# Head of a fused layer kernel: projection weights loaded in halves by two queues, other loads behind them, and the later tiles' normalisation moved

## The chip, the cores and the metric

One core of one Trainium2 chip. The metric is the device time of one launch in microseconds; everything, weights included, starts in HBM. The kernel before takes 723.18 us (median of 3 runs, 723.03 to 726.49).

## The reference, cut to what matters

An attention layer with fast weights, followed by a mixture-of-experts layer; x has 2048 rows of 256, all is fp32.

```
xn  = layernorm(x)                        # per row, 16 tiles of 128 rows
qkv = xn @ Wqkv ; small = xn @ [Wlr|Wm|Ws]  # one weight tile "wall", 820 columns with the gate's
for each of 16 chunks (128 rows), one after the other, carrying W0,W1,W2 and momenta:
    out   = W1 . (silu(W0 q) * (W2 q))          # with the weights as they stand
    dW0, dW1, dW2 from k, v and learning rates  # "key side", gradients
    M = dW + M * mean(momentum)
    W = renorm(W + newtonschulz5(M))            # 5 iterations of X X', A A, B X
windowed attention (128 back) beside it; sum of both @ Wo
feed-forward on xn: gate logits, top groups and experts, 8 of 32 experts per row,
    one shared expert (up, relu^2, down), sorted rows per expert group, fc2
output = x + attention part + feed-forward part
```

## The kernel before, in words

Five engines run five instruction streams written out by hand; they meet at semaphores, each engine in strict order. SP and ACT issue the DMAs, each on a queue of its own.

`body(i)` is the step of chunk i (0 to 15), and exists in every engine's stream. It has the key side (`k_side`), the query side (`q_side`, `q_gate`), gradients (`grads`, `grad`), the norm of the momentum (`sums`, `sum_copy`, `ss_pow`, `x_first`), and then 20 steps "st": four for each of 5 Newton-Schulz iterations. In st 0, 4, 8, 12, 16 something is turned or nothing is done, in st 1, 5, ... TensorE makes the Gram products and VectorE `Am` (`ns_a`), in st 2, 6, ... TensorE squares and VectorE makes `Mp` (`ns_m`), in st 3, 7, ... TensorE applies and ACT copies the new `XX` (`ns_x`). A dictionary `fill` says which other work an engine does after its part of a step: in st 4 the output norm (`q_norm`), in st 5 to 12 the projections and norms of chunk i+1 (`prep_...`), in st 11 to 17 attention. The last instructions renormalise the fast weights and turn them (`turn_w`, `w_T`), and the next chunk's key side waits for that.

Layer norm goes by groups n = 0 to 8: tile 0 alone, then tiles 2n-1 and 2n, last tile 15. For a group VectorE takes statistics (`ln_stats`, L1314 ff.), GpSimd raises variance+eps to the power -0.5 (`prep_rstd`, L431), VectorE makes the shift (`ln_shift`, L1337), ACT applies (`ln_apply`, L587), TensorE turns the result (`ln_turned`, L873), ACT copies it to `xnT_all` (`ln_xnT`, L595). `ln_turn(i, k, half)` places the turning in one of the slots of body 0: k counts 8 pairs of slots (`y_slot`, half 0; `h_slot`, half 1) among the steps. After each turning ACT applies the next group at once. `gate_pair(i, k, half)` places the router's eight groups of matmuls (`gate_rows`, TensorE; `gate_out`, ACT) in the same slots; the router's sort starts in body 1. Expert work fills the slots of later bodies.

Before body 0 stands the head, the same preparations for chunk 0: `ln_stats(0)`, `ln_first`, `ln_turned(0)`, `turn_w(0, g)`, then the projection (`prep_qk`, `prep_v`), silu, the norms of q and k by `prep_n8` (GpSimd) and `prep_qkn`, learning rates (`lr_a`, `lr_b`, `lr_c` around ACT's exp and ln, which lie in another table than sigmoid), the window copies and `prep_kl` (GpSimd). VectorE starts with 13 memsets, and the statistics of groups 1 to 4 are taken in the head, those of 5 to 8 in body 0. TensorE waits for `wall` and `rows` (bias rows) before the projection, and for all of the feed-forward weights before body 0.

Of the kernel before, what the change touches and what calls it, by code (L numbers as in the profile page):

```python
# [27 lines left out]
ALU = mybir.AluOpType  # L28
# [58 lines left out]
def build(nc, x, wall_d, rows_d, wo, fast_d, affine_d, fc1T, fc2T, e1T, e2T, upT, downT, ident_d, fixed_d, out):  # L87
# [10 lines left out]
    with ExitStack() as ctx:  # L98
# [170 lines left out]
        def per_group(name):  # L269
# [4 lines left out]
        e_const, e_later, e_ffn_w, e_ttw, e_init = (sem(n) for n in (  # L274
            "first_const_in", "later_const_in", "ffn_weights_in", "fast_weights_in", "init"))
# [33 lines left out]
        NCONST, NLATER, NFFN = 2, 3, 5  # L309
# [37 lines left out]
        def gate_pair(i, k, half):  # L347

            order = {(0, 1, 0): 0, (0, 2, 0): 1, (0, 3, 0): 2, (0, 4, 0): 3, (0, 5, 0): 4, (0, 6, 0): 5, (0, 7, 0): 6, (1, 0, 0): 7}
            return order.get((i, k, half))  # L350
# [5 lines left out]
        def _(sp):  # L356
            xv = x.rearrange("(t p) d -> p t d", p=P)
            sp.dma_start(x_all[:, 0, :], x[0:P, :]).then_inc(e_x0, 16)
            sp.dma_start(ident[:, :], ident_d[:, :]).then_inc(e_ident, 16)
            for dst, src in ((wall[:, :, :], wall_d[:, :, :]),  # L360
                             (rows[:, :], rows_d.partition_broadcast(P))):
                sp.dma_start(dst, src).then_inc(e_const, 16)
            sp.dma_start(x_all[:, 1:5, :], xv[:, 1:5, :]).then_inc(e_x1, 16)
            for dst, src in ((fixed[:, :, :], fixed_d[:, :, :]), (affine[:, :, :], affine_d[:, :, :]),
                             (wo_s[:, :, :], wo.rearrange("(k p) n -> p k n", p=P))):
                sp.dma_start(dst, src).then_inc(e_later, 16)
            sp.dma_start(x_all[:, 5:NT, :], xv[:, 5:NT, :]).then_inc(e_x2, 16)
            sp.wait_ge(e_init, 2)
# [54 lines left out]
        def _(pool):  # L423
# [94 lines left out]
            def body(i, last):  # L518
# [6 lines left out]
                k_u(i, 1)  # L525
                move(i, "key side", 4)
# [8 lines left out]
                if first:  # L535
                    fill[13] = [restore_mask]
                    for n, st in ((5, 1), (6, 4), (7, 6), (8, 8)):
# [19 lines left out]
            for g in range(G):  # L557
                row_pow(0, g)
            prep_n8(0)
            for n in range(1, 5):  # L560
                prep_rstd(n)
            window(0)
# [9 lines left out]
        def _(act):  # L572
            for g in range(G):
                act.dma_start(Wn[g][:, :, :], fast_d[g]).then_inc(e_ttw, 16)
            for dst, src in ((gf_s[:, :, 0:P], fc1T.rearrange("(k p) n -> p k n", p=P)),
                             (gf_s[:, :, P:P + E], wall_d[:, :, 3 * D + GATE:3 * D + SMALL]),
# [1383 lines left out]
```

## Time and profile before

| | |
|---|---|
| median of 3 runs | 723.18 us (723.03 to 726.49) |
| profiled execution | 722.96 us, its span 721.2 us |
| busy: TensorE / its weight load | 637.7 us (88%) / 527.1 us (73%) |
| busy: VectorE, ScalarE, GpSimd | 551.8 (77%), 386.8 (54%), 232.1 us (32%) |
| chain that ended last, by engine | PE 40%, DVE 36%, ACT 10%, POOL 6%, issue 5%, DMA 1% |
| DMA over the span | 75.52 MB, mean 105 GB/s |

PE is TensorE, PEld its weight load, DVE VectorE, ACT ScalarE, POOL GpSimd, SP the engine that only issues DMAs. Times in rows are microseconds from the start of the span; the 1.8 us between the span and the execution's own time lie around it. A row of a timeline can merge instructions that follow each other; what stands in brackets is how long the engine was idle just before and what ended that. No single engine is full and the chain runs over all of them, so what counts is which one ends last at each place.

### The profile page before, as it was taken

How to read it: one execution, taken by the hardware profiler on the slowest of the kernel's cores; microseconds unless marked ns; L12 is line 12 of the kernel's file. 1: busy time of each engine (PE TensorE's matmuls, PEld its weight loads, DVE VectorE, ACT ScalarE, POOL GpSimd, SP SyncE). 2: the span in 40 equal slices, each digit the busy share in tenths (PEclk: the TensorE clock that was granted, in tenths of full speed). 3: DMA queues.
4: the chain of work that ended last, by engine and by line, in shares of the span. 5: the costliest groups of instructions: out<-in, count | busy, mean ns of one | idle time of the engine just before them, and what ended most of it. 6: DMA issues, size and time to landing. Idle time of an engine off the chain costs nothing.

```text
span 721.2 us, 24642 instructions
## 1 busy us (share of the span) xinstructions
PE 637.7 (88%) x10081; PEld 527.1 (73%) x10081; DVE 551.8 (77%) x1878; ACT 386.8 (54%) x938; POOL 232.1 (32%) x296
## 2 busy tenths in 40 slices
PE   4688789878998899999999999999999999998865
PEld 2566577766776678878787887888878888786654
DVE  5876877798576687978879787897888878768554
ACT  2576353543553546656475665747647566452533
POOL 1522113117773221313113222131312213158730
PEclk9799979999999999999999999999999999998988
DMA  8300000220111125354454444454454553011211
GB/s 271 150 3 2 2 2 3 78 101 32 46 37 55 65 79 182 127 163 142 153 187 155 159 166 145 153 185 145 148 172 139 170 193 113 23 28 38 73 48 59
DMA packets 40160, 75.52 MB, mean 105 GB/s; under 512 B 9712, under 2 KB 24432, under 8 KB 40048
## 3 DMA queue, kind: packets, MB, share of 16 engines
q1 hardware_dynamic: 36224, 68.08, 29.0%
q0 software_dynamic: 2048, 4.33, 2.0%
q8 instruction: 80, 1.31, 0.7%
q10 hardware_dynamic: 1776, 1.54, 0.7%
q14 instruction: 32, 0.26, 0.1%
HBM read 64.73 MB, written 9.20 MB: 103 GB/s over the span
## 4 chain that ended last, share of the span: by engine, by line
PE 40%; DVE 36%; ACT 10%; POOL 6%; issue 5%; DMA 1%; SPq 0%; DVEq 0%; POOLq 0%
PE CC L860 13%; PE HB L860 9%; PE YB L860 8%; DVE hb L1782 6%; PE M L860 6%; ACT hb L583 3%; POOL r L429 3%; POOL xsrc L454 3%; ACT XX L583 3%; DVE Am L1485 2%; DVE sq L1497 2%; DVE Mp L1491 2%; DVE Wn L1503 1%; PE CC L1011 1%; DVE comb L1601 1%
## 5 line engine op out<-in xcount | busy, mean ns | idle before, releaser
L429 POOL TENSOR_TENSOR r<-r,half 128x3 f32<-128x3 f32 (+1 forms) x78 | 81.5, 1050 | 181.7 <-DVE r L1361 96.7
L583 ACT ACTIVATE hb<-HB 128x512 f32<-128x512 f32 x86 | 51.3, 597 | 67.4 <-PE HB L860 66.2
L583 ACT ACTIVATE XX<-CC 128x384 f32<-128x384 f32 (+1 forms) x150 | 63.1, 459 | 34.8 <-PE CC L860 33.9
L1782 DVE TENSOR_TENSOR hb<-hb,cwb 128x512 f32<-128x512 f32 x70 | 76.5, 1093 | 6.8 <-ACT hb L583 5.8
L860 PE MATMUL HB<-xsT,e_s 128*128 128x128 f32 x560 | 78.3, 283 | 1.7 <-issue 1.7
L860 PE MATMUL YB<-e_s,hb 128*128 128x128 f32 x560 | 77.4, 281 | 0.0
L860 PEld LDWEIGHTS YB<-e_s,hb 128*128 128x128 f32 x560 | 69.3, 191 | 7.1 <-issue 4.3
L860 PEld LDWEIGHTS HB<-xsT,e_s 128*128 128x128 f32 x560 | 67.9, 191 | 4.6 <-issue 1.8
L860 PE MATMUL CC<-XX,Mp 64*64 64x64 f32 x1800 | 63.2, 229 | 8.0 <-DVE Mp L1491 8.0
L860 PE MATMUL CC<-Am 64*64 64x64 f32 x1800 | 53.6, 236 | 18.1 <-DVE Am L1485 17.3
L860 PEld LDWEIGHTS CC<-Am 64*64 64x64 f32 x1800 | 41.4, 138 | 35.0 <-DVE Am L1485 29.9
L1491 DVE SCALAR_TENSOR_TENSOR Mp<-CC,rests 128x192 f32<-128x192 f32 x150 | 47.7, 353 | 25.0 <-PE CC L860 24.0
L860 PEld LDWEIGHTS CC<-XX,Mp 64*64 64x64 f32 x1800 | 50.7, 137 | 18.4 <-DVE Mp L1491 11.3
L1485 DVE TENSOR_TENSOR Am<-CC,shifts 128x192 f32<-128x192 f32 x150 | 47.5, 351 | 16.5 <-PE CC L860 14.8
L860 PE MATMUL M<-wall,xnT_all 128*128 128x512 f32 (+1 forms) x128 | 55.7, 541 | 2.2 <-DMA rows<-in_rows 1.4
L583 ACT ACTIVATE hb<-hb 128x512 f32<-128x512 f32 x86 | 54.0, 628 | 1.4
L860 PE MATMUL CC<-Mp,XX 64*64 64x64 f32 x1440 | 47.0, 223 | 0.3 <-issue 0.3
L478 POOL COPY akT<-akT 128x256 f32<-128x256 f32 x15 | 7.6, 505 | 122.9 <-issue 122.9
L429 POOL TENSOR_TENSOR r<-r,neghalf 128x4 f32<-128x4 f32 x16 | 16.2, 1011 | 88.9 <-DVE r L1545 88.9
L583 ACT ACTIVATE XT<-CC 128x256 f32<-128x256 f32 x30 | 11.3, 385 | 60.1 <-PE CC L958 60.1
L860 PEld LDWEIGHTS CC<-Mp,XX 64*64 64x64 f32 x1440 | 39.7, 139 | 0.4 <-issue 0.4
L860 PE MATMUL CC<-XX 64*64 64x64 f32 x1440 | 38.0, 231 | 2.0 <-ACT XX L583 2.0
(249 smaller groups left out, 1504.1 us busy)
## 6 DMA issues: line engine op xcount, KB each, us to landing
e_s<-in_e1T SPq DMA_DIRECT2D x35, 512.0 KB, 4.7
e_s<-in_e2T SPq DMA_DIRECT2D x35, 512.0 KB, 5.8
cwb<-tile_weights SPq DMA_DIRECT2D x35, 512.0 KB, 3.7
sorted_rows<-e_s SPq DMA_DIRECT2D x5, 476.0 KB, 9.8
xs<-sorted_rows SPq DMA_DIRECT2D x35, 68.0 KB, 5.5
sorted_out<-yo SPq DMA_DIRECT2D x35, 64.0 KB, 3.0
out<-xnT_all SPq DMA_DIRECT2D x8, 256.0 KB, 2.2
x_all<-in_x SPq DMA_DIRECT2D x1, 1408.0 KB, 14.7
```

Source lines behind the costliest of these rows:

```text
L429: return pool.tensor_tensor(dst, src, expo[:, 0:n], ALU.pow)
L454: pool.indirect_dma_start(xsrc[:, t, j, 0:P], None, y_d[:, :], bass.IndirectOffsetOnAxis(ap=dest_i[:, t, j:j + 1], axis=0)).then_inc(e_gat ...
L478: pool.tensor_copy(akT[:, :, 0, :], akT[:, :, 1, :])
L583: return nc.scalar.activation(out_, in_, func, **kw)
L860: return pe.matmul(out_, lhsT, rhs, start=start, stop=stop)
L1011: ins = pe.transpose(CA[g][0:HD, w * P:(w + 1) * P], Wn[g][:, w, :], ident[:, :])
L1485: nc.vector.tensor_tensor(Am[g][:, :, :], SQUARED[g] if it and g else PROD[g], shifts[:, it, :].unsqueeze(1).to_broadcast([P, 3, HD]), ALU ...
L1491: nc.vector.scalar_tensor_tensor(Mp[g][:, :, :], SQUARED[g] if it and not g else PROD[g], NS[it][2], rests[:, it, :].unsqueeze(1).to_broad ...
L1497: nc.vector.tensor_tensor(sq3[g][:, :, :], Wn[g][:, :, :], Wn[g][:, :, :], ALU.mult).then_inc(e_up[g], 1)
L1503: nc.vector.tensor_tensor(Wn[g][:, :, :], Wn[g][:, :, :], X[g][:, :, :], ALU.add).then_inc(e_up[g], 1)
L1601: nc.vector.tensor_tensor(comb[:, :], att[:, :], ttt[:, :], ALU.add).then_inc(e_comb, 1)
L1782: nc.vector.tensor_tensor(hb[u % RING][:, :, :], hb[u % RING][:, :, :], gate, ALU.mult).then_inc(e_hw, 1)
```

## The change

- **Loads.** `wall` is loaded in two halves (by its k index, 410 KB each), one on SP's queue behind tile 0 of x, one on ACT's queue ahead of the fast weights. The identity and `rows` stand behind SP's half. SP then waits until both halves have landed and issues everything else, the feed-forward weights too, which ACT issued before. TensorE waits for the halves only; `rows` is waited for by VectorE.
- **VectorE's start.** Four memsets (`akT`, `vw`, `beat`, `zero`) go behind the first normalisation and the Newton-Schulz constants; no engine waits for them until GpSimd's first window copy and SP's blank writes. The first statistics no longer wait for the memsets.
- **Head.** ACT loads the sigmoid table right after its three DMA issues. GpSimd does the window copies before the norms' power. The statistics of group 2 stand at the end of the head, those of 3 and 4 in body 0. VectorE copies the turned q and k (`first_qkT`) in place of ACT, and ACT applies group 1 behind its key side and gate sigmoid. Constants of the sort go to body 0, st 10.
- **Body 0.** Groups 1 to 8 are turned in the second halves of slots 0 to 7 (before: both halves of slot 0, then slots 1 to 6). ACT's `ln_apply` of groups 3 to 8 stands at fixed steps and no longer follows each turning; statistics and shifts are spread over st 0 to 17. TensorE does the first projection matmul of chunk 1 behind the momentum's sums. The router's eight groups go one slot later, (0,2) to (1,1).

```diff
 def ln_turn(i, k, half):
-    order = {(0, 0): 1, (0, 1): 2, (1, 1): 3, (2, 1): 4, (3, 1): 5, (4, 1): 6, (5, 1): 7, (6, 1): 8}
+    order = {(k, 1): k + 1 for k in range(PER)}
 def gate_pair(i, k, half):
-    order = {(0, 1, 0): 0, (0, 2, 0): 1, ..., (0, 7, 0): 6, (1, 0, 0): 7}
+    order = {((n + 2) // PER, (n + 2) % PER, 0): n for n in range(NT // 2)}
 # SP
 sp.dma_start(x_all[:, 0, :], x[0:P, :]).then_inc(e_x0, 16)
+sp.dma_start(wall[:, 0, :], wall_d[:, 0, :]).then_inc(e_wall, 16)
 sp.dma_start(ident[:, :], ident_d[:, :]).then_inc(e_ident, 16)
-wall, rows -> e_const ; x tiles 1-4 ; fixed, affine, wo ; x tiles 5-15
-sp.wait_ge(e_init, 2)
+rows -> e_const
+sp.wait_ge(e_wall, 32)
+x tiles 1-4 ; affine, fixed, wo ; gf_s (2) ; x tiles 5-15 ; up_s, down_s, fc2_s
+sp.wait_ge(e_init, 3)
 # GpSimd
 body(i): k_u(i, 0); k_u(i, 1)
+    if first: prep_rstd(2)
-    for n, st in ((5, 1), (6, 4), (7, 6), (8, 8)):   prep_rstd(n)
+    for n, st in ((3, 1), (4, 4), (5, 7), (6, 10), (7, 13), (8, 15)):   prep_rstd(n)
 head: prep_rstd(0); row_pow(0, g)
-    prep_n8(0); prep_rstd(1..4); window(0); prep_kl(0)
+    pool.wait_ge(e_init, 3); window(0); prep_n8(0); prep_rstd(1); prep_kl(0)
 # ACT
+act.dma_start(wall[:, 1, :], wall_d[:, 1, :]).then_inc(e_wall, 16)
 fast weights
-gf_s (2), up_s, down_s, fc2_s
+act.preload_act_table_set("sigmoid_and_others")
 extra(i, k, half):  ln_xnT(n)
-    if n < NL - 1: ln_apply(n + 1)
+    if n == 1: ln_apply(2)
 body(i): k_side(i, 0); k_side(i, 1); gate_sig(i)
+    if i == 0: ln_apply(1)
+    if i == 0:
+        fill[7], fill[8] = [prep_small(m), prep_sq8(m), y_slot(i, 3)], []
+        ln_apply(n) for n, st in ((3, 2), (4, 5), (5, 9), (6, 12), (7, 16), (8, 18))   # 9, 12: first in the step
 head:
-    w_T(0, g); prep_vT(0); table exp/ln; lr_exp(0); prep_qkT(0); lr_ln(0); table sigmoid; ln_apply(1)
+    w_T(0, g); prep_vT(0); table exp/ln; lr_exp(0); lr_ln(0); table sigmoid
 # TensorE
-body: prep_qk(m); sums(i, 0); sums(i, 1)
+body 0: sums(0, 0); sums(0, 1); prep_qk(m)
 head:
-pe.wait_ge(e_const, 16 * NCONST)
+pe.wait_ge(e_wall, 32)
 # VectorE
-beat, zero, akT, vw memset at the start; dve.wait_ge(e_init, 2)
+def blanks():   akT, vw, beat, zero memset, then e_init
+def first_qkT():
+    dve.wait_ge(e_pnqk, 1)
+    nc.vector.tensor_copy(qkT, M1).then_inc(e_qkT, 1)
 body 0:
+    ln_shift(2) ahead of x_first
-    ln_stats (5, 0), (6, 2), (7, 4), (8, 6);  ln_shift (5, 2), (6, 4), (7, 6), (8, 8)    # (group, st)
+    ln_stats (3, 0), (4, 2), (5, 6), (6, 8), (7, 12), (8, 14)
+    ln_shift (3, 2), (4, 5), (5, 9), (6, 12), (7, 14), (8, 17)    # shifts first in the fill
+    fill[10] += sort_consts
 head:
+    blanks() behind ns_consts()
-    ln_stats(1); ln_stats(2); prep_qkn; lr_b; ln_shift(1); ln_shift(2); ln_stats(3); ln_stats(4); lr_c; ln_shift(3), (4)
+    ln_stats(1); prep_qkn; lr_b; first_qkT(); ln_shift(1); lr_c; ln_stats(2)
```

## Rows read from the trace of the kernel before

**Rows 1.** Chain of waits, 0 to 110 us; columns: start, us, what.

```profile
2.13 7.86 DMA rows<-in_rows
```

**Rows 2.** Timeline of the head, all engines: start, us, engine, line, operation, [idle before].

```profile
4.53 0.43 DVE L1324 BATCH_NORM_STATS2 st<-x_all 128x6 f32<-128x256 f32 x1
...
6.64 0.29 PEld L869 LDWEIGHTS M<-ident,xn 128*128 128x128 f32 x2 [6.64 <-issue]
...
10.03 0.50 PEld L860 LDWEIGHTS M<-wall,xnT_all 128*128 128x128 f32 x2 [1.88 <-DMA rows<-in_rows]
```

**Rows 3.** DMA issues, 0 to 26 us: size, median us from issue to landing.

```profile
wall<-in_wall SPq DMA_DIRECT2D x1, 820.0 KB, 6.5
...
x_all<-in_x SPq DMA_DIRECT2D x1, 128.0 KB, 2.6
...
fc_s<-in_fc2T ACTq DMA_DIRECT2D x1, 128.0 KB, 13.2
rows<-in_rows SPq DMA_DIRECT2D x1, 74.0 KB, 7.9
ident<-in_ident SPq DMA_DIRECT2D x1, 64.0 KB, 2.5
```

**Rows 4.** Windows of the head; last columns: granted clock, DMA share, GB/s.

```profile
0.70:3.50 2.80, 0.00 (x0) 0.00 (x0) 2.52 (x10) 0.00 (x0) 0.15 (x1) 1.00 0.66 157
3.50:5.50 2.00, 0.00 (x0) 0.00 (x0) 1.72 (x8) 0.00 (x0) 0.00 (x0) 1.00 0.68 132
5.50:10.00 4.50, 1.94 (x8) 1.31 (x8) 3.07 (x17) 1.67 (x2) 2.03 (x3) 1.00 0.87 285
10.00:18.00 8.00, 5.69 (x12) 2.73 (x12) 2.77 (x11) 3.41 (x9) 0.33 (x2) 0.96 1.09 361
```

**Rows 5.** Timelines of GpSimd and VectorE, the norms of q and k in the head.

```profile
17.93 1.64 POOL L429 TENSOR_TENSOR r<-r,half 128x8 f32<-128x8 f32 x1 [7.67 <-DVE r L1361]
```

```profile
20.36 0.17 DVE L1365 TENSOR_SCALAR r<-r 128x8 f32<-128x8 f32 x1
```

**Rows 6.** Timeline of ACT, end of the head.

```profile
22.69 0.60 ACT L583 ACTIVATE qkT<-M 128x512 f32<-128x512 f32 x1 [2.40 <-PE M L927]
...
24.70 1.09 ACT L583 ACTIVATE xn<-x_all,shift,rstd 128x256 f32<-128x256 f32 x2
25.70 0.52 ACT L583 ACTIVATE ks<-CC 128x128 f32<-128x128 f32 x2
```

**Rows 7.** Groups by form on VectorE: first 26.2 to 30.6 us (body 0), then 73 to 75.9 us (body 1); columns: busy us, mean ns.

```profile
L1421 DVE SCALAR_TENSOR_TENSOR kt<-ks,kt 128x128 f32<-128x128 f32 x2 | 1.3, 628 | 0.0
```

```profile
L1421 DVE SCALAR_TENSOR_TENSOR kt<-ks,kt 128x128 f32<-128x128 f32 x2 | 0.6, 302 | 0.0
```

**Rows 8.** Timelines of GpSimd and TensorE, body 0 up to the Newton-Schulz steps.

```profile
26.58 1.24 POOL L470 TENSOR_TENSOR kl<-qkn,lr 128x256 f32<-128x256 f32 x2
```

```profile
29.86 0.30 PE L860 MATMUL CC<-kl,dga 128*64 128x64 f32 x2 [1.05 <-DVE dga L1430]
...
34.27 1.25 PE L860 MATMUL YB<-gf_s,xnT_all 128*128 128x160 f32 x8
```

**Rows 9.** Timelines of GpSimd and VectorE, body 0, st 3 to 5.

```profile
42.82 0.70 POOL L435 TENSOR_TENSOR rstd<-veps,neghalf 128x2 f32<-128x2 f32 x1
```

```profile
43.55 0.16 DVE L1342 SCALAR_TENSOR_TENSOR shift<-mv,rstd 128x2 f32<-128x2 f32 x1 [1.78 <-POOL rstd L435]
...
44.82 0.75 DVE L1324 BATCH_NORM_STATS2 st<-x_all 128x6 f32<-128x256 f32 x2
```

**Rows 10.** Timelines of VectorE and TensorE, body 0, st 13 and 17.

```profile
56.81 0.74 DVE L1485 TENSOR_TENSOR Am<-CC,shifts 128x192 f32<-128x192 f32 x2 [0.59 <-PE CC L860]
```

```profile
61.54 0.83 PE L860 MATMUL CC<-XX 64*64 64x64 f32 x24 [0.57 <-ACT XX L583]
```

**Rows 11.** Timeline of TensorE, body 1, the first turning.

```profile
80.50 0.30 PE L957 MATMUL CC<-ident,XX 128*64 128x128 f32 x1 [0.77 <-DVE XX L1468]
```

**Rows 12.** Windows, body 1: columns as in rows 4.

```profile
80.00:100.00 20.00, 15.56 (x316) 12.00 (x320) 16.99 (x111) 8.69 (x20) 3.10 (x3) 0.74 0.01 2
```

More of the change, by code:

```diff
@@ L525, in body @@
                 k_u(i, 1)
+                if first:
+                    prep_rstd(2)
                 move(i, "key side", 4)
@@ L536, in body @@
                     fill[13] = [restore_mask]
-                    for n, st in ((5, 1), (6, 4), (7, 6), (8, 8)):
+                    for n, st in ((3, 1), (4, 4), (5, 7), (6, 10), (7, 13), (8, 15)):
                         fill[st] = fill.get(st, []) + [lambda n=n: prep_rstd(n)]
@@ L558, in _ @@
                 row_pow(0, g)
+            pool.wait_ge(e_init, 3)
+            window(0)
             prep_n8(0)
-            for n in range(1, 5):
-                prep_rstd(n)
-            window(0)
+            prep_rstd(1)
             prep_kl(0)
@@ L725, in extra @@
                     ln_xnT(n)
-                    if n < NL - 1:
-                        ln_apply(n + 1)
+                    if n == 1:
+                        ln_apply(2)
                 n = gate_pair(i, k, half)
@@ L781, in body @@
                     h_sq(i - 1, PER - 1)
+                else:
+                    ln_apply(1)
                 y_slot(i, 0)
@@ L798, in body @@
                         15: [lambda: lr_ln(m), lambda: probs_T(i)], 16: [lambda: h_sq(i, 5)], 17: [to_sigmoid]}
+                if i == 0:
+                    fill[7], fill[8] = [lambda: prep_small(m), lambda: prep_sq8(m), lambda: y_slot(i, 3)], []
+                    for n, st in ((3, 2), (4, 5), (5, 9), (6, 12), (7, 16), (8, 18)):
+                        fill[st] = [lambda n=n: ln_apply(n)] + fill.get(st, []) if st in (9, 12) else fill.get(st, []) + [lambda n=n: ln_apply(n)]
                 if i == SORT_STEP:
@@ L836, in _ @@
             lr_exp(0)
-            prep_qkT(0)
             lr_ln(0)
             act.preload_act_table_set("sigmoid_and_others")
-            ln_apply(1)
             body(0, False)
@@ L1222, in body @@
                 h_slot(i, 0)
-                prep_qk(m)
+                if i:
+                    prep_qk(m)
                 sums(i, 0)
                 sums(i, 1)
+                if i == 0:
+                    prep_qk(m)
                 prep_qk_more(m)
@@ L1769, in route, with sort_consts @@
                 return [lambda: biased().then_inc(e_rt, 1)] + [after(step) for step in rest]
+            def sort_consts():
+                nc.vector.tensor_scalar(before[:, :], fixed[:, 2, :], 0.0, None, ALU.is_lt)
+                dve.wait_ge(e_jrow, 1)
+                nc.vector.tensor_copy(jrow_f[:, :], jrow[:, :])
+                nc.vector.tensor_scalar(jrow_p[:, :], jrow[:, 0:NT], float(P), None, ALU.mult).then_inc(e_jrow, 1)
             def h_weight(i, k):
@@ L1905, in _ @@
             ln_stats(1)
-            ln_stats(2)
             prep_qkn(0)
             lr_b(0)
+            first_qkT()
             ln_shift(1)
-            ln_shift(2)
-            ln_stats(3)
-            ln_stats(4)
             lr_c(0)
-            ln_shift(3)
-            ln_shift(4)
+            ln_stats(2)
             routing = route()
             dve.wait_ge(e_later, 16 * NLATER)
-            nc.vector.tensor_scalar(before[:, :], fixed[:, 2, :], 0.0, None, ALU.is_lt)
-            dve.wait_ge(e_jrow, 1)
-            nc.vector.tensor_copy(jrow_f[:, :], jrow[:, :])
-            nc.vector.tensor_scalar(jrow_p[:, :], jrow[:, 0:NT], float(P), None, ALU.mult).then_inc(e_jrow, 1)
             body(0, False)
```

52 lines of the change are left out of this document (27 added, 25 removed).

## Prediction

> **What bounds the kernel now.** I read the page first: TensorE is busy 88% of the span, VectorE 77%, and the chain that ended last alternates between them, with 1% of DMA in all. The change touches no work outside the first 120 us or so, so I then read the chain of waits there. Its one long piece is the head's wait for the bias rows, 7.86 us from issue to the first projection at 10.03 [rows 1, 2]. From then on the chain is one engine waiting for the next, in bodies 0 and 1 too. The 14 bodies behind them wait for the fast weights of the body before, so a microsecond gained ahead of them should arrive at the end whole, and one lost too. I take the effect at the Newton-Schulz steps of body 1 as the effect on the time.
>
> **The front: gain 1.3 us.** TensorE needs, in this order, the identity and the normalised tile 0 (its turning is at 6.64), the fast weights, and the projection weights. Turning and fast-weight turning keep it from 6.64 to about 8.35, so 1.7 us before the projection even without a wait; it then stands until 10.03 for `rows` [rows 2], though `wall` landed 6.5 us after its issue at 1.66, so at 8.16 [rows 3]. Taking `rows` out of the wait gives 1.7 us at most with the turnings where they are. Four memsets leave VectorE's start; tile 0 lands 2.6 us after its issue [rows 3], which is SP's first, at some 3.3, so the statistics could start 1.2 us before their 4.53 [rows 2], and the turning at 5.5.
> But the identity now stands behind half of `wall` on SP's queue, the fast weights behind the other half on ACT's. What must come in before the projection is 128 + 820 + 64 + 192 KB and, partly, 74 KB of rows: 1.31 MB. The queues moved 157 GB/s up to 3.5, 132 up to 5.5 and 285 after that [rows 4]. With the dip at 3.5 to 5.5 kept, that is 0.44 + 0.26 MB by 5.5 and the other 0.61 in 2.1 us: 7.6. Without it 0.87 MB in 3.05 us: 6.5. I take 7.0 for identity, fast weights and both halves; TensorE then needs 1.7 us: the projection starts at 8.7, 1.3 us earlier. Ends: by 5.6 (nothing but the turning limits) the gain is 2.7; with the landing left at 8.16 it is 0.1.
> By the Trainium skill's page "DMA: Bandwidth & Descriptors" (section "Issuing engines are not separate DMA queues") transfers started by two engines run on the same 16 DMA engines and interleave, and only the time to start them is saved. It gives the halving by itself no gain: by that rule what helps is only that less is queued around the halves. The case that the landing does not move is a rival below.
> ACT's earlier table load costs nothing: ACT has nothing else until tile 0 is turned. The moved memsets stand behind the constants, which wait for the identity; by my estimate they end near 9.5, the fast weights' norms near 13, and VectorE is not wanted for chunk 0 before about 14. That cover has 1 us left, and past it the loss is one to one.
>
> **Norms in the head: gain 0.8 us.** GpSimd's power ends at 19.57, but VectorE is in the statistics of group 2 until 20.36 [rows 5]. These go behind. GpSimd's three window copies, now ahead of the power, fit into its idle 7.67 us before it [rows 5]. `first_qkT` on VectorE costs about the 0.60 us of ACT's copy [rows 6]; it delays nothing that is late, and ACT can switch back its table ahead of it.
>
> **Key side to first turning of body 0: gain 1.5 us.** ACT's table load and the applying of group 1 (24.70) hold back its key-side copies until 25.70 [rows 6]; without them these wait for TensorE and start some 0.6 us earlier. VectorE's 12 steps of the key side are slower here than in body 1: L1421 takes 628 ns against 302, and over all six lines of that view (two instructions each) it is 5.1 against 3.6 us [rows 7], while GpSimd makes `kl` at the same time, from 26.58 on [rows 8]. With learning rates and group 1 out of the way `kl` is made some 2 us before the key side, so about 1.4 of these 1.5 us go. And one group of router matmuls, 1.25 us [rows 8], leaves the place ahead of the first turning. That is 3.3 us if all were on one chain. TensorE limits it: of its time here only the 1.05 us that it waits for `dga` and the 1.25 us of the router can go [rows 8], 2.3 us; gradient, gate sigmoid and the turning of group 1 are new in a row before the projection of chunk 1, and VectorE makes the statistics of group 3 before the first `Am`. I take off 0.8 for these. Bounds: 0 (TensorE waits for ACT's `ln_apply(1)` all that it had waited for `dga`) to 2.3.
>
> **Steps 3 to 5 of body 0: gain 1.0 us.** VectorE stands 1.78 us for group 6's power, which GpSimd starts only at 42.82 behind the output norm's; then it takes 1.1 us for the statistics of group 7 at 44.82 ahead of `Am` [rows 9]. After the change neither is there: the output norm goes on when its own power ends, 0.7 us earlier, and `Am` comes 1.8 us earlier. What is late next is new: shift 4 stands behind `Am` on VectorE, ACT applies group 4 behind that (about 1.1 us, as at 24.70 [rows 6]), and TensorE turns group 4 ahead of its apply matmuls. I work this out as 0.8 us of waiting. Bounds: 0 to 1.8.
>
> **Steps 7 to 19: loss 0.5 us.** ACT's applies no longer stand ahead of `XX`, for which TensorE waited 0.57 us at 61.54 [rows 10]. Against it: group 5's apply waits for a shift behind `Am` in the same way, the statistics of group 7 (1.1 us) stand ahead of an `Am` before which VectorE was idle only 0.59 us [rows 10], and two applies stand ahead of the last `XX`. Sort constants fit an idle stretch ahead of the mask. Bounds: -1.5 to +0.6.
>
> **Body 1: loss 0.4 us.** A router group now stands ahead of the first turning: 1.25 us on TensorE, of which 0.77 were idle [rows 8, 11]. Bounds: -0.9 to 0.
>
> **Weights for body 0: nothing.** TensorE waits for all feed-forward weights before body 0, which it will reach when q and k are copied: 23.29 before [rows 6], less 2.1, so 21.2. They used to land by 17.2 (issue 4.03 + 13.2 [rows 3]). Now 3.84 MB follow the halves on one queue: from 7.9 at 361 GB/s [rows 4] that is 10.6 us, 18.5, with 2.7 us to spare.
>
> Sum: 1.3 + 0.8 + 1.5 + 1.0 - 0.5 - 0.4 = 3.7 us. The profiled execution took 722.96, which is 0.2 under the median of 723.18; 722.96 - 3.7 = 719.3, and against the median it would be 719.5. I say 719.4.
>
> **Rivals.** About 0.5% (3.6 us) can be told from no change.
> - *The halves land no earlier* (0.17). For it: both queues feed the same engines, and the 2 us at 132 GB/s came with few bytes in flight beside `wall` [rows 4]; against: less is queued beside them. The front gives 0.1: 720.6.
> - *Body 0 gives its gain back* (0.18). The chain shift, apply, turning, which ACT and VectorE now have at fixed steps, costs 1.8 in place of 0.8 at group 4 and again 0.8 more at 5 and 7: 719.4 + 1.8 = 721.2. For it: each apply waits for a shift that stands behind `Am`; against: slack of TensorE in router matmuls.
> - *Clock* (0.12). Body 1 runs 10 of its us at half clock (0.74 over 80 to 100 [rows 12]), after a stretch in which TensorE waited for VectorE. If that falls away, some 2 us more are gained: 717.4.
> - *Slower* (0.08): TensorE's wait for the feed-forward weights before body 0. They all follow both halves now. It decides from a landing at 21.2, and eats the whole gain of 3.7 from 24.9; that is 3.84 MB at under 226 GB/s from 7.9. At the 157 GB/s that the head's first stretch had [rows 4] they land at 32.4, and the kernel takes 719.4 + 11.2 = 730.6; at 200 GB/s they land at 27.1, 5.9 us late, which makes 725.3. Against: 361 GB/s as soon as large loads run.
> - The forecast itself has 0.45, with 717.9 to 720.9 as its own range.
>
> **Numbers.** Faster by over 0.5% is a time under 719.6: a little over half of the forecast's case, nearly all of the clock's, little of the others, with half of a further case that the front gains near its 2.7: 0.46. Slower by over 0.5% (over 726.8) is the last rival, and part of it stays below: with what is unforeseen 0.07. Same 0.47. The range reaches from the clock's case with a better front, 715.8, to 722.9.
>
> **What would show it.** The projection's first weight load near 8.7; VectorE's L1421 in body 0 near 300 ns; the first turning of body 0 3.6 us earlier than before; no wait of VectorE for `rstd` in steps 3 to 5; TensorE waiting for ACT's `xn` at the turning of group 4; body 1's key side 4.1 us earlier; no wait of TensorE for `fc2` or `down` between 17 and 21. If the projection starts after 9.5, or body 1 comes under 2 or over 6 us earlier, the sum is wrong at the step where the difference arises.

## The result, and the profile after

| | before, same chip | after |
|---|---|---|
| median | 723.32 us (4 runs, 723.03 to 726.49) | 717.34 us (4 runs, 716.14 to 718.73) |
| ratio of the runs | | 0.989 (95% interval 0.986 to 0.993), so 7.7 us less |
| profiled execution, its span | 722.96, 721.2 us | 717.34, 715.3 us |
| mean granted clock in it | 0.971 | 0.980 |

Faster. The two medians of the table differ by 6.0 us, the ratio says 7.7 (its interval is 5.4 to 10.2 us), and all runs of both kernels together, 70 and 10, say 8.3: some twice the 3.7 us of the sum. The time lies in the forecast range, the size of the gain was wrong. Six more runs of the changed kernel gave 717.36 us (ratio 0.989, 0.985 to 0.992).

**Where the loads land now.** Windows of the changed kernel's head, columns as in [rows 4].

```profile
0.70:3.50 2.80, 0.00 (x0) 0.00 (x0) 1.81 (x10) 1.28 (x1) 0.15 (x1) 1.00 0.50 123
3.50:5.50 2.00, 0.00 (x0) 0.00 (x0) 0.51 (x2) 0.00 (x0) 0.00 (x0) 1.00 1.03 392
5.50:10.00 4.50, 2.90 (x10) 2.20 (x11) 3.52 (x18) 0.38 (x1) 0.57 (x1) 1.00 0.59 197
```

Its DMA issues, columns as in [rows 3]:

```profile
wall<-in_wall ACTq DMA_DIRECT2D x1, 410.0 KB, 4.0
wall<-in_wall SPq DMA_DIRECT2D x1, 410.0 KB, 5.0
...
x_all<-in_x SPq DMA_DIRECT2D x1, 128.0 KB, 4.2
...
fc_s<-in_fc2T SPq DMA_DIRECT2D x1, 128.0 KB, 7.6
...
ident<-in_ident SPq DMA_DIRECT2D x1, 64.0 KB, 5.0
```

The dip to 132 GB/s between 3.5 and 5.5 us [rows 4] is gone: 392 GB/s. Tile 0 of x pays for it, 4.2 us in place of 2.6, and the identity lands with the half ahead of it, 5.0 in place of 2.5. Timelines of VectorE and of TensorE's weight loads, columns as in [rows 2]:

```profile
4.96 0.43 DVE L1336 BATCH_NORM_STATS2 st<-x_all 128x6 f32<-128x256 f32 x1 [2.29 <-DMA x_all<-in_x]
```

```profile
7.07 0.29 PEld L875 LDWEIGHTS M<-ident,xn 128*128 128x128 f32 x2 [7.07 <-DMA ident<-in_ident]
7.35 1.25 PEld L1017 LDWEIGHTS CC<-ident,Wn 128*64 128x64 f32 x6
8.63 0.55 PEld L866 LDWEIGHTS M<-wall,xnT_all 128*128 128x128 f32 x2
```

Statistics and turning are both 0.43 us later than before, 2.11 us apart in both kernels: it is tile 0 that is late, not the identity, though the profile names the identity. Nothing waits for `wall`: behind the turnings TensorE goes on into the projection at 8.63, 1.40 us before the 10.03 of [rows 2].

**Norms and key side.** Timeline of GpSimd, then of VectorE; the first answers to [rows 5], the second to [rows 5, 7].

```profile
13.89 0.40 POOL L484 COPY akT<-akT 128x256 f32<-128x256 f32 x1 [1.26 <-ACT raw L587]
14.23 0.86 POOL L485 COPY vw<-vw 128x256 f32<-128x256 f32 x1
15.16 0.47 POOL L487 COPY vw<-raw 128x256 f32<-128x256 f32 x1
16.30 1.64 POOL L435 TENSOR_TENSOR r<-r,half 128x8 f32<-128x8 f32 x1 [0.67 <-DVE r L1373]
```

```profile
13.92 0.91 DVE L1363 TENSOR_TENSOR sl<-raw,sig 128x512 f32<-128x512 f32 x1
14.76 0.61 DVE L1368 TENSOR_TENSOR sl<-raw,sig 128x256 f32<-128x256 f32 x1
...
17.97 0.17 DVE L1377 TENSOR_SCALAR r<-r 128x8 f32<-128x8 f32 x1 [0.23 <-POOL r L435]
...
23.84 0.29 DVE L1437 SCALAR_TENSOR_TENSOR kt<-ks,kt 128x128 f32<-128x128 f32 x1
...
34.49 0.65 DVE L1501 TENSOR_TENSOR Am<-CC,shifts 128x192 f32<-128x192 f32 x2
```

VectorE takes up the norms 2.39 us earlier (17.97 for 20.36). Its `kt` product takes 0.29 us in place of the 0.628 of [rows 7]. `sl` takes 0.91 us while GpSimd copies the windows; before, at 15.79 without them, it took 0.68.

**Body 0 and body 1.** Timeline of TensorE; answers to [rows 8, 9, 10, 11].

```profile
21.21 1.19 PE L866 MATMUL CC<-WT,qkT 128*128 128x256 f32 x2 [0.93 <-DMA fc_s<-in_fc2T]
...
31.46 0.30 PE L963 MATMUL CC<-ident,XX 128*64 128x128 f32 x1
...
38.01 0.66 PE L875 MATMUL HB<-ident,xn 128*128 128x128 f32 x4 [0.86 <-ACT xn L587]
...
41.77 0.66 PE L875 MATMUL HB<-ident,xn 128*128 128x128 f32 x4 [0.75 <-ACT xn L587]
...
48.06 0.66 PE L875 MATMUL HB<-ident,xn 128*128 128x128 f32 x4 [0.70 <-ACT xn L587]
...
56.47 0.83 PE L866 MATMUL CC<-XX 64*64 64x64 f32 x24 [0.53 <-ACT XX L587]
...
76.25 0.30 PE L963 MATMUL CC<-ident,XX 128*64 128x128 f32 x1 [0.28 <-DVE XX L1484]
```

The new waits for `xn` are there, 0.86, 0.75 and 0.70 us at the turnings of groups 3, 4 and 5. One window of body 1, which answers to [rows 12]:

```profile
80.00:100.00 20.00, 15.21 (x356) 12.43 (x352) 16.81 (x112) 9.91 (x25) 2.64 (x2) 0.91 0.01 3
```

The stretch at half clock in body 1 lasted 10.2 us before (from 89.1) and lasts 3.4 us in this profile (from 90.0). A second profile of the same kernel, below, has 6.8.

How much earlier each place comes than before, from the starts of its instruction in both traces:

| place | before | after | gained by then | of it here |
|---|---|---|---|---|
| projection, first matmul | 10.03 | 8.84 | 1.2 | 1.2 |
| `z` (VectorE, behind the projection) | 15.69 | 13.83 | 1.9 | 0.7 |
| norms of q, k (VectorE) | 20.36 | 17.97 | 2.4 | 0.5 |
| first turning of body 0 | 35.35 | 31.46 | 3.9 | 1.5 |
| apply of iteration 1, body 0 | 47.53 | 42.36 | 5.2 | 1.3 |
| key side of body 1 | 71.56 | 66.50 | 5.1 | -0.1 |
| `q_ms` of body 1 | 84.94 | 79.89 | 5.1 | 0.0 |
| `comb`, end of attention, body 1 | 108.89 | 103.17 | 5.7 | 0.7 |
| `comb` of body 15 | 714.63 | 708.78 | 5.9 | 0.1 |

### The profile page after: what moved, and what is told of

Its sections match the earlier page's. It is cut to its first block, busy times and chain, and to the rows that moved or that the text cites. A ratio compares the mean times of both kernels' runs of the same rounds, so it can differ in the third digit from the quotient of the medians.

```text
span 715.3 us, 24646 instructions
## 1 busy us (share of the span) xinstructions
PE 633.8 (89%) x10081; PEld 524.3 (73%) x10081; DVE 550.9 (77%) x1879; ACT 386.7 (54%) x937; POOL 232.5 (32%) x296
## 4 chain that ended last, share of the span: by engine, by line
PE 38%; DVE 36%; ACT 10%; POOL 7%; issue 5%; DMA 2%; SPq 1%; DVEq 0%; POOLq 0%; ACTq 0%
PE CC L866 13%; PE HB L866 9%; PE YB L866 7%; DVE hb L1804 7%; PE M L866 5%; POOL xsrc L460 4%; ACT hb L587 3%; POOL r L435 3%; ACT XX L587 3%; DVE Am L1501 2%; DVE sq L1513 2%; DVE Mp L1507 2%; DVE Wn L1519 2%; PE CC L1017 1%; DVE comb L1617 1%
```

## The experiments

Ratios are to the kernel before, run on the same chip; "body 1" is the first matmul of its key side in the profiled execution, at 71.56 before and 66.50 after.

**Parts.** One kernel has the front of the changed kernel and everything else of the kernel before, the other the reverse.

```diff
# front alone: SP's order, ACT's half, VectorE's start, TensorE's waits of after; the rest of before
# rest alone: router slots, window copies, first_qkT, LN groups of after; the front of before
```

> The kernel before with the front of the change alone: halves of the projection weights on two queues, other loads behind them, four memsets later, sigmoid table early; layer norm, router and norms in their old places. Theory A (work by the trace of after: front 1.9 us up to the bias add at 13.83, norms 0.5, key side and router slot 1.5, steps of body 0 1.2, the rest clock): projection starts at about 8.6, bias add near 13.8, body 1's first turning 1.9 us earlier than before, time about 1.9 us under before (721.3). Rival B (the forecast's parts hold but the front is worth more, since all the unforeseen gain arose there): body 1 comes 4 us earlier. Rival C (the rest undoes the front, TensorE waits for other things): 0.

Measured: 722.34 us (10 runs), ratio 0.996 (0.993 to 0.999); body 1 at 70.20, 1.36 us gained.

> The kernel after with the old front: weights whole, bias rows in TensorE's wait, loads and memsets as before; everything else as after. Theory A: projection at 10.0, body 1 3.1 us earlier than before, time 3.1 to 4 us under before (719.8), and with e1 the two sum to the whole change. Rival B: 1 us. If the parts do not add up (sum of both more than 1 us off the 5.1 us at body 1), a part covers for another.

Measured: 721.59 us (10 runs), ratio 0.993 (0.990 to 0.995); body 1 at 69.43, 2.13 us gained. The parts make 3.5 us, the whole 5.1. The missing 1.6 us arise ahead of `z`: there it is 1.35 gained by the front alone, 1.05 *lost* by the rest alone, and 1.86 gained by the whole. From `z` to body 1 it is 0.0, 3.2 and 3.2: there the parts add up. In the rest alone the projection began 0.29 us later than before and its eight matmuls took 5.62 us, against 4.86 before, 4.78 in the front alone and 4.14 in the changed kernel, with no load awaited between them.

The length of the projection follows the clock. In all 16 traces of this case it is 2.83 us plus half of the time from its first matmul to the moment at which the trace first notes the full clock, within 0.11 us. Between traces with the same code up to there it varies by almost 1 us: 3.85 to 4.78 us in the eight with the halves, 4.86, 5.32 and 5.62 in the three with the old front. So the 1.6 us are at least in part chance of single executions; by the ratios of ten runs each the parts bring 2.8 and 5.2 us, together 8.0, as much as the whole. Over these traces `z` comes at 14.11 us on average (13.62 to 14.78) with the halves and at 16.05 (15.69 to 16.74) without: 1.9 us.

**Halves or whole.**

```diff
-sp.dma_start(wall[:, 0, :], wall_d[:, 0, :]).then_inc(e_wall, 16)
+sp.dma_start(wall[:, :, :], wall_d[:, :, :]).then_inc(e_wall, 16)   # ACT issues none of it
```

> The kernel after with the projection weights as one transfer on SP's queue behind tile 0, the rest unchanged. If it is what is no longer queued beside them that counts, and not the two queues, they land within 0.5 us of after's 6.2 and the projection starts within 0.5 us of 8.63; the turnings of tile 0 and the fast weights then start earlier, as nothing stands ahead of the fast weights. If the two queues count, the weights land 1 us or more later (over 7.2) and the time is 1 us above after.

Measured: 716.90 us (4 runs), ratio 0.988 (0.983 to 0.993). DMA issues and TensorE's weight loads of this kernel:

```profile
wall<-in_wall SPq DMA_DIRECT2D x1, 820.0 KB, 5.0
...
x_all<-in_x SPq DMA_DIRECT2D x1, 128.0 KB, 2.7
...
ident<-in_ident SPq DMA_DIRECT2D x1, 64.0 KB, 4.7
```

```profile
6.37 0.29 PEld L874 LDWEIGHTS M<-ident,xn 128*128 128x128 f32 x2 [6.37 <-DMA ident<-in_ident]
6.64 1.24 PEld L1016 LDWEIGHTS CC<-ident,Wn 128*64 128x64 f32 x6
7.92 0.55 PEld L865 LDWEIGHTS M<-wall,xnT_all 128*128 128x128 f32 x2
```

820 KB on one queue land in 5.0 us, as 410 KB do there beside ACT's half; the projection starts 0.71 us earlier, and body 1 0.26, since the projection took 4.64 us here for 4.14. The two queues bring nothing, and cost tile 0 of x 1.5 us (4.2 for 2.7). That all loads share the same DMA engines whichever engine starts them, and that two issuers save only the time to issue, is what the Trainium skill's page "DMA: Bandwidth & Descriptors", section "Issuing engines are not separate DMA queues", says, and here the traces agree.

What no run isolates is the plainest part of the front: taking `rows` out of TensorE's wait. In the kernel before `wall` was there at 8.16 and the last weight load of the turnings ended at 8.15 (6.91 + 1.24), so by an estimate from these two the projection could have begun near 8.2 with the old loads, before the 8.63 of the changed kernel.

**Identity first, the wall whole behind it** (with the shifts of a later experiment):

```diff
 sp.dma_start(ident[:, :], ident_d[:, :]).then_inc(e_ident, 16)
 sp.dma_start(wall[:, :, :], wall_d[:, :, :]).then_inc(e_wall, 16)
```

> The kernel after with the projection weights whole on SP's queue, the identity ahead of them, and the shifts of groups 4 and 5 ahead of Am (e6). In e3 tile 0 of x landed at 3.4 but its turning waited until 6.4 for the identity behind the weights. Theory: turning near 5.3, fast weights next, projection at about 7.1 (after 8.8), the bias add 1.0 to 1.5 us earlier than in after, and 1.2 us more from the shifts: body 1 2.2 to 2.8 us earlier than in after, time 715 at the mean clock of after. Rival: without the two queues the weights land so late (6.5 and more) that the projection starts only at 7.8; body 1 1.5 us earlier.

Measured: 718.02 us (6 runs), ratio 0.990 (0.986 to 0.994). The turning comes at 5.83, but `wall` lands 6.9 us after its issue in place of 5.0 and the projection starts at 8.60: what the small load gains, the large one loses. The kernel with the statistics one step later, below, has the same order; there `wall` took 6.3 us and the weight load of the projection is at 8.03, against 7.92, 8.06 and 7.96 in the three kernels with the whole `wall` first. With the old front, where `wall` stands behind the identity too but nothing is held back, it took 6.1 to 6.5 us in three traces: holding the other loads back shows no gain for `wall`.

Body 1 comes at 66.61, 0.1 us later than in the changed kernel, for which 2.2 to 2.8 earlier was expected and 1.5 by the rival. The projection took 5.20 us, and TensorE now does wait for the feed-forward weights, which land at 22.45 because SP issues them only when `wall` is there:

```profile
22.54 1.22 PE L865 MATMUL CC<-WT,qkT 128*128 128x256 f32 x2 [1.50 <-DMA fc_s<-in_fc2T]
```

From the norms to the key side it is 3.81 us here and 3.24 in the changed kernel: 0.57 of real waiting.

**A late landing of the feed-forward weights**, the mechanism of the slower rival.

```diff
-up_s, down_s, fc2_s issued behind x tiles 5-15
+up_s, down_s, fc2_s issued behind the five blank writes
```

> The kernel after with the up, down and fc2 weights (1.15 MB) issued behind the five blank writes (2.4 MB). In after fc2 lands at 20.4 and TensorE starts body 0 at 21.2, when q and k are copied. Here it lands about 6 us later, near 26, and TensorE waits. Theory (a microsecond ahead of body 0 arrives whole at the end): body 0 and body 1 start 5 us later than in after, time 5 us above it, 722 to 723. Rival: part of it is taken up later (the sort, the scatter or the expert loads wait for something of their own): body 1 5 us late, but the last bodies under 3 us.

Measured: 723.49 us (10 runs), ratio 0.997 (0.995 to 0.999). Timeline of TensorE's weight loads:

```profile
27.01 0.50 PEld L866 LDWEIGHTS CC<-WT,qkT 128*128 128x128 f32 x2 [6.79 <-DMA fc_s<-in_fc2T]
```

The key side stands 5.80 us later than in the changed kernel, body 1 5.81, the end 5.99, the median 6.1 (5.4 to 5.8 by the ratios): a microsecond ahead of body 0 arrives whole. On the way the distance grows to 8.5 us at body 3 and shrinks again, by half-clock stretches at other places.

**The window copies** back behind the norms.

```diff
-pool.wait_ge(e_init, 3); window(0); prep_n8(0); prep_rstd(1)
+prep_n8(0); prep_rstd(1); pool.wait_ge(e_init, 3); window(0)
```

> The kernel after with GpSimd's three window copies of the head behind the norms' power, where the kernel before had them (after the power and group 1's). In after VectorE's silu products took 0.91 and 0.61 us while GpSimd copied, against 0.68 and 0.42 in before. Theory: with the copies away they take 0.68 and 0.42 again, the sum of squares comes 0.2 us earlier, and nothing waits for the copies: body 1 comes 0.2 us earlier than in after (by the trace). Rival: the copies then lie on kl's way and collide with first_qkT and lr_c: 0.3 us later.

Measured: 717.72 us (4 runs), ratio 0.988 (0.983 to 0.993). From `z` to the norms' sums it is 1.47 us against 1.70, so the copies do cost 0.23; from the power to the key side 0.12 of it come back. Net 0.1.

**The router's old slots.**

```diff
-order = {((n + 2) // PER, (n + 2) % PER, 0): n for n in range(NT // 2)}
+order = {(0, 1, 0): 0, (0, 2, 0): 1, ..., (0, 7, 0): 6, (1, 0, 0): 7}
```

> The kernel after with the router's eight groups in their old slots, (0,1) to (1,0). Theory A: the first turning of body 0 comes 1.2 us later (32.7), most of it stays until body 1 (0.8 to 1.2), and body 1 gives nothing back, since there the group in slot (1,1) lies beside VectorE's scaling of the attention inputs: time 1 us above after, 718.3. Rival (my forecast's term: slot (1,1) costs 0.4 us in body 1): 0.4 of it comes back at body 1's first turning to Am, so 0.6 or less remains.

Measured: 719.41 us (10 runs), ratio 0.992 (0.989 to 0.994). The first turning of body 0 is 1.16 us later than in the changed kernel (0.14 of it at `z` already), the apply of iteration 1 1.71, body 1 1.71, and the first `Am` of body 1 1.72: what the group costs ahead of the turning of body 0 it does not cost ahead of that of body 1. In the changed kernel VectorE's `XX` is what TensorE awaits there, 0.28 us at 76.25. The rival, and with it the forecast's term for body 1, fell. The median is 2.05 us above the changed kernel's, not 1.

**Shifts ahead of `Am`**, for groups 4 and 5:

```diff
-(4, 5), (5, 9)                      # shift first in the fill of st 5, 9, behind Am
+fill[4] += [ln_shift(4)] ; fill[8]: ln_shift(5) ahead of its last entry
```

> The kernel after with the shifts of groups 4 and 5 ahead of Am (ends of steps 4 and 8) and not behind it. In after TensorE waited 0.75 us (group 4) and 0.70 us (group 5) for ACT's apply, ACT for the shift. Theory: ACT applies group 4 behind its copies of q and k, group 5 in its idle stretch; both waits go, the apply matmuls of iterations 1 and 2 come 0.7 and 0.9 us earlier, of which about 0.5 reaches body 1 (the rest is taken by router matmuls and ACT's XX copies), by the trace. Rival: nothing reaches body 1, since the attention mask and statistics of group 7 decide at step 13.

Measured: 717.69 us (4 runs), ratio 0.989 (0.984 to 0.994). TensorE's waits for `xn` fell from 0.75 to 0.20 and from 0.70 to none, body 1 comes 0.89 us earlier, 1.24 if its later front is allowed for. The time is the same: this kernel has its 10.2 us at half clock in body 1 again, from 84.0, and 43.3 us of them in all against 30.2. The shifts need not be the reason: the kernel with the window copies behind the norms has the changed kernel's shifts, and 10.2 us too (from 84.8).

**Statistics of group 7 one step later**, on top of identity, wall and shifts as above:

```diff
-(7, 12)      # ln_stats(7) ahead of Am of st 13
+(7, 13)      # and its shift last but one in st 14
```

> As e12, with the statistics of group 7 in step 13 behind the attention maximum (in step 12 they stand ahead of Am and delay the maximum), and its shift at the end of step 14. Theory: maximum and exp 0.9 us earlier, XX of iteration 3 0.4 us earlier, body 1 0.3 us earlier than in e12. Rival: the statistics delay Mp by 0.6 us instead, body 1 same or later than in e12.

Measured: 718.18 us (5 runs), ratio 0.989 (0.986 to 0.993). Body 1 comes 1.42 us before that of the changed kernel. From the key side of body 0 on the statistics bring 0.83 us, more than the 0.3 expected, and the wait for the feed-forward weights takes 1.1 back (norms to key side 4.37 us). Again the time is not less; 43.3 us at half clock.

So two kernels waited less on the chain and took the same time. Either the work gained was not worth what the trace said, or the clock gave it back.

**TensorE kept busy.** Six matmuls that nobody reads, in body 1 alone:

```diff
+# in `if i == SORT_STEP:`, that is body 1
+def warm():
+    for _ in range(3): mm(HB[:, :], xnT_all[:, 0, 0, :], wall[:, 0, 0:2 * D])
+fill[5] += [warm] ; fill[9] += [warm]
```

> The kernel after with six matmuls of 512 columns whose result nobody reads, three in step 5 and three in step 9 of body 1, where TensorE waits 1.9 and 1.7 us for VectorE's Am. They add 3.2 us of TensorE work, most of it in those waits. Theory (TensorE's idle stretches bring the half-clock stretches): the half-clock stretch near 90 us of the trace goes, mean clock up by 0.003 to 0.005, time 0.5 to 1 us under after. Rival 1 (the clock falls by something else): the stretch stays, time same or up to 1 us above. Rival 2: the matmuls delay the squares by 0.5 us each, time 1 us above, stretch or not.

Measured: 717.23 us (6 runs), ratio 0.988 (0.985 to 0.992), mean clock over the runs 0.979. The changed kernel once more, in the same batch:

> The kernel after, unchanged, beside runs of the kernel before on the same chip. So far the runs of before have a median of 726.04 us at a mean granted clock of 0.970 (25 runs, 722.1 at 0.978 to 728.4 at 0.967), those of after 717.34 at 0.977 (4 runs). Theory: of the measured gain of 7.7 us some 5.3 are work moved off the chain (seen at one clock) and 2 to 2.5 are a higher mean clock, which the change itself brings (fewer half-clock stretches in bodies 1 to 3): mean clock of after 0.975 to 0.978 again, times 716 to 720, 7 to 8 us under before in the same rounds. Rival: the higher clock was luck of four runs: mean 0.970 to 0.973, 5.5 us under before.

Measured: 717.36 us (6 runs), mean clock 0.974, between what the theory and its rival gave for the clock; the time is the theory's. On the changed kernel the matmuls bring nothing that can be measured in the time, though the mean clock rises by 0.004 and no half-clock stretch is left in body 1. From its key side to `comb` body 1 takes 36.93 us with them, 36.67 and 36.65 in the two profiles of the changed kernel.

These two profiles are of one kernel and show how far a single one can be trusted. One window of body 1, in the second profile of the changed kernel and in the kernel with the window copies behind the norms, which has the same code there; the first profile had 0.91:

```profile
80.00:100.00 20.00, 15.70 (x352) 12.86 (x352) 16.72 (x116) 9.92 (x25) 2.65 (x2) 0.83 0.01 3
```

```profile
80.00:100.00 20.00, 16.43 (x347) 13.43 (x351) 16.99 (x112) 9.35 (x23) 2.65 (x2) 0.74 0.01 3
```

The same code has 3.4, 6.8 and 10.2 us at half clock in body 1, which takes 36.67, 36.65 and 37.32 us. In the second profile another stretch, 3.4 us from 239.6, falls into body 4 and costs 1.0 us there. It is 1.3 us behind the first at body 5 and 1.2 ahead at the end.

> The kernel BEFORE with the six unread matmuls in steps 5 and 9 of body 1. Means so far: before 0.9696 granted clock (36 runs, mean 725.7 us), after 0.9754 (10 runs, 717.4); in the profile of before body 1 has a half-clock stretch of 10.2 us after those waits of TensorE, in the one of after 3.4 us. Theory (TensorE's waits in body 1 are what makes the clock fall there, and their coming at another time is what the change gains beyond the work it moves): no half-clock stretch near 89 us, mean clock 0.973 or more, time 1.5 us or more under before. Rival: the clock of bodies 0 and 1 is lost elsewhere: mean clock 0.970 as before, time same or 0.3 above.

Measured on the kernel before: 723.70 us (12 runs, mean clock 0.976) against 727.00 (23 runs, 0.969), ratio 0.997 (0.995 to 1.000), so 2.0 us less by the ratio (0.3 to 3.6) with more work. The pair of profiled executions does not show where: 722.96 and 722.99 us, and the end of body 1 comes 0.95 us later with the matmuls, although 3.4 us at half clock are left there for 10.2.

**Everything, with the clock left to itself and then not.** The first kernel has the wall whole ahead of the identity, both shifts, the statistics, and no wait of TensorE for all feed-forward weights; the second adds the six matmuls in body 1.

```diff
-pe.wait_ge(e_ffn_w, 16 * NFFN)      # ahead of body 0; the users wait for their weights themselves
```

> The changed kernel with four edits: the projection weights loaded whole by SP ahead of the identity, the shifts of groups 4 and 5 ahead of Am, the statistics of group 7 one step later, and no wait of TensorE for all feed-forward weights before body 0 (their users wait for them). Theory that work off the chain arrives whole: the key side of body 1 starts 0.26 + 1.24 + 0.84 = 2.3 us before the 66.50 of the changed kernel, at 64.2, and the end of the profiled execution lies 2.3 us earlier up to what its half-clock stretches differ; median 717.4 - 2.3 = 715.1 at the same mean clock. Rival: that less idle or other idle places of TensorE take it back through the clock: body 1 at 64.2 all the same, median 716.5 to 718, and a mean clock at least 0.003 below that of the changed kernel.

Measured: 717.61 us (6 runs), ratio 0.991 (0.987 to 0.994), mean clock 0.970; body 1 at 64.36, as computed. The gain of 2.1 us by then is 1.0 at the end of body 1, which has 10.2 us at half clock, and a loss of 0.7 at body 5, behind a half-clock stretch of 3.4 us from 237.5 that the first profile of the changed kernel has not.

> The kernel of the run before with six matmuls in every body that nobody reads (three of 128x512 in step 5, three in step 9), as tried on both kernels. Theory that the clock is a share of the time of its own: mean clock up by 0.004 to 0.007, own work 0.26 us in body 1, median 1.5 to 2 us below the run before it. Rival: the clock is already as high as the changed kernel's, the matmuls bring nothing: median within 0.5 us of the run before it, at the same mean clock.

The six matmuls stand in body 1 alone here too, not in every body as the expectation has it; the trace shows them in two groups of three, two instructions for each, and none behind 88.5 us:

```profile
79.47 2.74 PE L865 MATMUL HB<-wall,xnT_all 128*128 128x512 f32 x6
85.71 2.74 PE L865 MATMUL HB<-wall,xnT_all 128*128 128x512 f32 x6
```

Measured: 714.86 us (6 runs), ratio 0.987 (0.984 to 0.991), mean clock 0.980; body 1 at 63.87. One window of body 1 in the first kernel and then in the second, columns as in [rows 4]:

```profile
76.00:106.00 30.00, 24.68 (x500) 20.52 (x497) 23.86 (x137) 14.77 (x34) 6.66 (x10) 0.83 0.01 3
```

```profile
76.00:106.00 30.00, 27.21 (x502) 20.79 (x503) 24.56 (x144) 14.99 (x34) 7.48 (x10) 1.00 0.01 3
```

The rival held for the first kernel: 2.1 us less work ahead of body 1, a clock lower by 0.004 than the changed kernel's (0.974 over its six later runs, 0.975 over all ten), the same time. It does not stand alone: the four kernels with the shifts ahead of `Am` and no added matmuls have a mean clock of 0.971 (21 runs), the changed kernel and the three that differ from it in whole `wall`, window copies or router slots 0.975 (28 runs), and the one with the late weights, where TensorE waits 6.79 us for them, 0.969 (10 runs).

The second kernel only adds work and is 2.75 us faster; every one of its runs but one is faster than all six of the first. So the matmuls gain time. But the two profiled executions place only a third of their 2.9 us where the matmuls are: 0.5 us are there before body 1 (a projection of 3.40 us for 4.78), 0.9 arise in body 1, whose 10.2 us at half clock are gone, and 1.5 in body 4, where the stretch from 237.5 is absent. Whether six matmuls in body 1 can do anything about a stretch 150 us later was not tried; it also comes and goes without them. It is the lowest ratio of all kernels here. Its median lies 8.9 us under that of the kernel before (723.80, 11 runs beside it). Against the changed kernel, which did not run beside it, it is 2.5 us less by the medians and 1.1 by the ratios; against the changed kernel with the matmuls 2.4 and 0.7. The ratios' intervals overlap in both, so that the work taken off the chain arrives at the end is likely and not shown.

## Why the prediction was right in kind and wrong in size

- **Front, forecast 1.3 us, measured 1.9.** The start of the projection was right (8.63 for 8.7), though by another way: the halves and the identity were there by 6.2 and 6.7, and it is tile 0, landing 1.6 us later than before, that holds the turning to 7.07. The term left out how long the projection itself takes. Its eight matmuls took 4.14 us against 4.86, which is all of the missing 0.6. Their length follows when the clock rises, and that varies with the same code by almost as much. All three traces with the old front lie above all eight with the halves, so the edit may have a part in it; that was not separated.
- **Norms, forecast 0.8, measured 0.5.** The copies of the windows were put at nothing, because they fit into GpSimd's idle time [rows 5]. They did, and made VectorE's `sl` slower beside them (0.91 for 0.68 us).
- **Key side to first turning, forecast 1.5, measured 1.5.** VectorE's L1437 takes 0.29 us as in body 1. With the router's old slots 1.0 us of it is gone, so its group was the larger part.
- **Steps 3 to 5, forecast 1.0, measured 1.3.** The new wait at group 4 is 0.75 us at 41.77, for which 0.8 stood. The one of 0.86 us at 38.01 is group 3's, which the sum did not have. `Am` of iteration 1 comes 2.1 us earlier all the same (45.89 and 39.91), where 1.8 stood; the router's groups help, since with their old slots this stretch is 0.55 us longer. `rstd` is awaited by nobody any more.
- **Steps 7 to 19, forecast -0.5, measured -0.1.** The wait for group 5's `xn` exists, 0.70 us, and the wait for `XX` that it was to be set against is still there (0.53 for 0.57 [rows 10]). The statistics of group 7 do delay `Am` of iteration 3, whose lead falls from 5.7 to 4.5 us, and 0.6 us of that come back by `Am` of iteration 4. Moving them one step brought 0.8 us, so they do cost time there; what gives it back in the changed kernel was not separated.
- **Body 1, forecast -0.4, measured 0.** The group in slot (1,1) was charged with what TensorE lacked of idle time [rows 8, 11]. The turning waits for VectorE's `XX`, and its first half is turned behind the group at 75.59; what was lost there, 0.6 us of the gain at `XT`, was back at the first `Am` (82.46 before, 77.39 now) and at `q_ms`.
- **Feed-forward weights, forecast nothing, measured 0.1.** They landed at 20.4 and not at 18.5, so the spare was 0.8 us and not 2.7. The trace puts 0.93 us of waiting down to them, but without this wait the key side follows the norms by 3.14 us and with it by 3.24; TensorE was waiting for the turned q and k, copied by 21.0. In the two kernels with the identity first the same wait cost 0.6 and 1.1 us.
- **The clock, forecast 0 with a rival of 0.12, is the step that failed.** The sum took the clock of one execution of before as given. The runs show instead 0.7 us in the projection, which follows the clock's rise, and in body 1 0.65 us from the stretch that went from 10.2 to 3.4 us, against the rival's 2 us for its going altogether; the same code with 10.2 us takes 37.32 us for body 1 as the kernel before does. That these two profiles stand so far apart is partly luck. The rest does not show in them: over all batches the kernel before has a mean clock of 0.970 (70 runs, mean 725.7 us) and the changed kernel 0.975 (10 runs, 717.4). A line through all 173 runs of the 15 kernels with a level of its own for each falls by 4.2 us for each 0.01 of mean clock (5.0 within the kernel before, 2.2 within the changed one); by it 2.4 of these 8.3 us go with the clock and 5.9 do not, near the 5.1 to 5.9 us that the table of places shows. It is a correlation, and not a price: on the changed kernel six matmuls raised the mean clock by 0.004 and brought nothing.

The balance: 4.1 us were forecast by the key side of body 1 and 5.1 came, the projection's length and the steps being the difference; 0.4 of loss in body 1 did not come; 0.8 came behind it, most of it clock. That is 5.9 in the spans and 5.6 between the two profiled executions. The other 2 us up to the 7.7 of the ratio lie in what a single execution does not show: the one of before that was profiled, at 722.96, is 2.8 below the mean of its kernel, and the median of 723.18 that the forecast started from is 2.5 below it: those first runs were lucky ones. The head's half-clock stretch is shorter as well (6.8 us from 18.3 for 10.2 from 17.4), and what it gave to the norms and the key side was not separated from the edits.

Of the rivals, "body 0 gives its gain back" fell: it gave back 0.1. "The halves land no earlier" fell too: both were there by 6.2 us, before it was 8.2; but as the whole tile on one queue is as well, the halving has no part in it. The slower rival's price was right, one to one, and its condition stayed 0.8 us away.

What stays open is how much of the higher clock is the change's doing, and what sets the half-clock stretch of body 1: 3.4 and 6.8 us in two profiles of the changed kernel, 10.2 in kernels with less waiting ahead of it but also in one with as much. The Trainium skill's page "TensorE: Matmul & The Clock Gate", section "What's actually happening", has half speed as the default and activity as what releases it. The last pair of kernels agrees (0.83 and 1.00 in the same window, with six matmuls in it between them); which of TensorE's pauses in body 1 brings the stretch was not tried.

## What to carry to other kernels

Work a chain gain out step by step, but price it against several runs with their clocks, and profile the same kernel twice before a difference of a microsecond between two profiles is explained: a microsecond off the chain can come back as half-clock time, and three good edits here showed nothing in the time by themselves. To bring a head forward, first look at what the wait contains, then at the order within the queue, not at the number of queues: a small load behind a large one lands with it. A stall that the profile names for a load may be worth nothing, as this one for `fc_s`, or all of it, as in the kernel with the identity first; compare the landing with the end of the other things awaited.

## What the runs showed of the hardware

- **Six added matmuls, in one of 16 bodies, made kernels faster**: by 2 us on the kernel before (clock 0.969 to 0.976) and 2.75 us on the kernel with all edits (0.970 to 0.980); by nothing on the changed kernel (0.974 to 0.979).
- **A half-clock stretch costs by where it falls**: 3.4 us of it cost 1.0 to 1.5 us in body 4 (44.6 us without, 45.6 to 46.1 with), and in body 1 6.8 us cost no more than 3.4 (36.65 and 36.67 us), 10.2 us 0.65 more (37.32).
- **A small load rides with the large one ahead of it on its queue**: 64 KB took 2.5 us ahead, 5.0 behind 410 KB, 4.7 behind 820 KB. Ahead, it cost the 820 KB behind it 1.9 us in one trace and 1.3 in another.
- **Two large loads on two queues delay what is issued beside them**: tile 0 of x, 128 KB, landed after 4.1 to 4.6 us in the eight traces with the halves, after 2.5 to 2.9 in the other eight.
- **The first matmuls vary from run to run without any wait**: the projection's eight took 3.40 us in one trace, 5.62 in another. The trace notes the clock's full level first at 9.4 us in the one and at 16.1 in the other; over 16 traces the length is 2.83 us plus half of the time until then.
- **VectorE and GpSimd side by side**: VectorE's 128x512 product took 0.91 us beside GpSimd's copies and 0.68 without; its 128x128 product with a scalar 0.63 beside GpSimd's `kl`, 0.29 without.
